# Turning the expert tiles' rows: from TensorE transposes to VectorE's 32x32 block transpose

## The chip, the cores and the metric

One core of one Trainium2 chip runs the whole kernel in one launch. The metric is the time of one execution on the device in microseconds (us), lower is better. A profile is one more execution, recorded instruction by instruction. The engines are named as in the profile: PE is TensorE (PEld its weight loads), DVE is VectorE, ACT is ScalarE, POOL is GpSimd, SP is SyncE, which here only issues DMAs.

## What is computed

The reference is two gated residual layers over `x` of shape (16, 256, 512), all float32. The first is an mLSTM attention, whose part of the kernel the change does not touch. The second is a mixture of experts, for T = 4096 tokens of width H = 512, with E = 16 experts of inner width I = 256 and the best 2 experts of each token:

```
scores = softmax(x @ router_w.T);  topk_w, topk_idx = top_k(scores, 2);  topk_w /= sum(topk_w)
g = einsum('th,ehi->tei', x, expert_gate);  u = einsum('th,ehi->tei', x, expert_up)
a = silu(g) * u
y = einsum('tei,eih,te->th', a, expert_down, gates)
s = silu(x @ shared_gate) * (x @ shared_up) @ shared_down
out = x + tanh(g_ffn) * (y + s)
```

## The kernel before

The kernel has three stages. Stage 1 (0 to about 620 us of the span) goes over the 16 batches: attention, router, the shared expert, and a scatter of each token's normalized row to two places of `routed_x` in HBM, so that the rows of one expert lie together. Stage 2, the expert stage (about 620 to 1027 us), takes those rows in 79 tiles of 128 tokens. Stage 3 combines the experts' outputs with the rest and does the shared expert of four batches that were put off.

Every engine has its own program, written out by hand, and runs it in that order. An instruction that waits for a semaphore holds up all that stand behind it on its engine. The semaphores are counted by tile (`t.n`).

A product of full float32 accuracy is made of three float32r products: an operand is split in a rounded high part and a low part, which is the rest, and the three are high x high, high x low, low x high (`PARTS`). So an activation that goes into a product is first turned (features onto partitions), rounded by one engine, and the rest is made by another.

For a tile `t` of the expert stage the steps are:

- `load_tile` (SP; the first four by ACT at L912): one DMA of 128 rows of 2 KB into `xt`, a ring of four.
- `turn_rows` (PE, L1248): four 128x128 transposes into PSUM bank `t.par`.
- `copy_x` (ACT, L917): PSUM to `xtT[:, 0]`, rounded. `rest_x` (DVE, L1829): PSUM minus that, to `xtT[:, 1]`.
- `gate_up` (PE, L1260): 12 products (four 128-feature chunks `c`, three parts each) into bank 2 or 3.
- `tanh_gate` (ACT, L921) and `silu` (DVE, L1811, L1815) give the activation `act_a`.
- `turn_act` (PE, L1269): two transposes; `copy_actT` (DVE, L1822, L1824): its high and low part.
- `down` (PE, L1278): six products; `copy_y` (ACT, L927) and `store_y` (ACT's DMA queue).

One step of PE is: `turn_rows(t+2)`, `turn_act(t)`, `gate_up(t+1)`, `down(t)`. One step of DVE is: `copy_actT(t)`, `rest_x(t+2)`, `silu(t+1)`.

The weights of expert `e` are loaded by POOL's DMAs into a staging area and split by POOL itself into the ring `w_ring` of two experts: a multiplication by one that rounds (L648), then a subtraction for the low part (L651), each over 128x3072 elements. POOL starts when the last `down` of expert `e-2` is done. The parts of experts 0 and 1 are made before the loop by ACT, DVE (L1805) and POOL (L631, L634):

```
g.tensor_tensor(w_ring[:, k, 0, :], stage[k], one[:, :].to_broadcast([P, EW]), ALU.mult)
g.tensor_tensor(w_ring[:, k, 1, :], stage[k], w_ring[:, k, 0, :], ALU.subtract)
```

Between its second and third step DVE also makes the table of places of the outputs once (seven short operations, L1845 to L1855, "the slot steps").

## Time and profile before

| | us |
|---|---|
| Time, median of 3 runs (lowest, highest) | 1141.49 (1140.75, 1142.49) |
| Span of the profiled execution | 1133.2 |
| Median less span: what lies around the span | 8.3 |
| PE busy | 1025.1 (90% of the span) |
| DVE busy | 761.3 (67%) |
| POOL busy | 419.3 (37%) |
| ACT busy | 386.4 (34%) |

The profiled execution has no time of its own beside its span; 8.3 us is the difference to the median of the timed runs, and a change of the span is taken as the same change of the time. Matmuls overlap in the pipeline, so the busy time of PE says that it never stood idle, not that it did useful work all the time. The page's releasers are inferred: a wait is put down to the event that came last.

### The profile page before, as it was taken

Reading aid. Unit: us, or ns where it says so; the run is one execution under the profiler, and the core shown is the slowest. Engines: PE = TensorE matmul, PEld = TensorE weight load, DVE = VectorE, ACT = ScalarE, POOL = GpSimd, SP = SyncE. Lnnn points to the kernel's source line nnn. Section 1 sums busy time; section 2 is a strip of 40 time slices with the busy share of each in tenths; the row PEclk is TensorE's granted clock in tenths of the full one; section 3 lists DMA queues with packets and bytes.
Section 4 is the critical chain, followed back from the end, with each engine's and each line's share of the span. In section 5 each row is a group of like instructions: output and inputs, shape, how many; then the busy total and the mean of one; then the engine's idle time right before and its main releaser. Section 6 shows DMA issues by size and latency. Waiting matters only on the chain.

```text
span 1133.2 us, 20738 instructions
## 1 busy us (share of the span) xinstructions
PE 1025.1 (90%) x6395; PEld 859.9 (76%) x6395; DVE 761.3 (67%) x1983; ACT 386.4 (34%) x854; POOL 419.3 (37%) x309
## 2 busy tenths in 40 slices
PE   4689999999999988989895599999999999999882
PEld 2578988898889877868684478888888888887661
DVE  2888889888888887878766544444444444444766
ACT  2644444444443444435421123233323333231010
POOL 4010221222112221222215536558656676204675
PEclk9889999999999998989976899999999999999986
DMA  7340210222012202120107744564555554836888
GB/s 259 149 164 1 76 71 9 82 75 76 20 56 76 75 38 80 52 94 38 75 38 260 265 135 167 176 207 158 170 195 193 168 176 149 325 112 186 285 288 272
DMA packets 60036, 155.60 MB, mean 137 GB/s; under 512 B 7296, under 2 KB 7296, under 8 KB 58016
## 3 DMA queue, kind: packets, MB, share of 16 engines
q0 software_dynamic: 18448, 69.22, 17.6%
q1 hardware_dynamic: 29008, 62.93, 16.1%
q10 hardware_dynamic: 12480, 22.16, 5.5%
q8 instruction: 59, 0.97, 0.4%
q14 instruction: 41, 0.34, 0.1%
HBM read 93.46 MB, written 60.82 MB: 136 GB/s over the span
## 4 chain that ended last, share of the span: by engine, by line
PE 80%; DVE 5%; issue 4%; DMA 4%; POOL 3%; ACT 2%; SPq 1%; ACTq 0%; POOLq 0%; DVEq 0%; another core or an unknown queue 0%
PE bank L1260 19%; PE bank L1125 12%; PE bank L1278 10%; PE bank L1030 5%; PE bank L1136 5%; PE bank L1053 4%; PE bank L993 4%; PE bank L1248 3%; POOL w_ring L694 3%; PE bank L1074 3%; PE bank L1077 3%; PE bank L1075 3%; PE bank L1322 2%; PE bank L1062 2%; PE bank L1269 2%
## 5 line engine op out<-in xcount | busy, mean ns | idle before, releaser
L1260 PE MATMUL bank<-w_ring,x2nT 128*128 x948 | 241.8, 404 | 1.7 <-DVE x2nT L1829 1.7
L1260 PEld LDWEIGHTS bank<-w_ring,x2nT 128*128 128x128 f32 x948 | 174.3, 191 | 37.7 <-issue 2.4
L1125 PE MATMUL bank<-x2nT,w_ring 128*128 128x256 f32 x1152 | 148.5, 285 | 0.0
L563 POOL DMA_INDIRECT routed_x<-x2n,slot_u x64 | 65.8, 1029 | 222.8 <-DVE slot_u L1593 207.0
L1125 PEld LDWEIGHTS bank<-x2nT,w_ring 128*128 128x128 f32 x1152 | 141.0, 191 | 0.3
L1811 DVE SCALAR_TENSOR_TENSOR ctxT<-ctxT,bank 128x256 f32<-128x256 f32 x79 | 33.3, 421 | 138.7 <-ACT ctxT L921 138.7
L1278 PE MATMUL bank<-w_ring,sh_actT 128*128 x474 | 123.7, 396 | 1.1 <-DVE sh_actT L1824 1.1
L648 POOL TENSOR_TENSOR w_ring<-area,one 128x3072 fp32r<-128x3072 f32 x14 | 74.2, 5303 | 115.5 <-PE bank L1278 115.5
L1278 PEld LDWEIGHTS bank<-w_ring,sh_actT 128*128 128x128 f32 x474 | 88.9, 188 | 22.5 <-issue 1.4
L651 POOL TENSOR_TENSOR w_ring<-area,w_ring 128x3072 fp32r<-128x3072 f32 x14 | 95.6, 6832 | 2.5 <-POOL w_ring L648 2.5
L921 ACT ACTIVATE ctxT<-bank 128x256 f32<-128x256 f32 x79 | 30.3, 384 | 189.9 <-PE bank L1260 189.9
L694 POOL DMA_INDIRECT w_ring<-routed_y,y_slot x64 | 66.5, 1039 | 34.9 <-issue 19.6
L1136 PE MATMUL bank<-w_ring,sh_actT 128*128 128x512 f32 x288 | 75.2, 411 | 1.3 <-issue 1.3
L1455 DVE SCALAR_TENSOR_TENSOR area<-bank,area 128x384 f32<-128x384 f32 x128 | 66.0, 551 | 14.5 <-PE bank L1053 7.8
L927 ACT COPY cs_in<-bank 128x512 f32<-128x512 f32 x79 | 46.3, 586 | 84.7 <-PE bank L1278 79.1
L1822 DVE CAST sh_actT<-bank 128x256 fp32r<-128x256 f32 x79 | 33.5, 424 | 60.9 <-PE bank L1269 60.9
L570 POOL TENSOR_TENSOR x_rstd<-x_var,minus_half 128x2 f32<-128x2 f32 x16 | 12.8, 797 | 152.4 <-DVE x_var L1518 152.4
L1053 PE MATMUL bank<-area,ctxT 64*128 64x256 f32 (+1 forms) x512 | 67.1, 379 | 0.0
L778 ACT ACTIVATE area<-bank,key_log 128x256 f32<-128x256 f32 x128 | 61.1, 478 | 10.8 <-PE bank L1064 10.2
L1136 PEld LDWEIGHTS bank<-w_ring,sh_actT 128*128 128x128 f32 x288 | 53.8, 194 | 13.0 <-issue 1.5
L1248 PE MATMUL bank<-ident,x2n 128*128 128x128 f32 x316 | 48.4, 277 | 12.5 <-issue 7.0
L1053 PEld LDWEIGHTS bank<-area,ctxT 64*128 64x128 f32 x512 | 51.0, 206 | 11.3 <-issue 5.5
(224 smaller groups left out, 2052.8 us busy)
## 6 DMA issues: line engine op xcount, KB each, us to landing
routed_y<-cs_in ACTq DMA_DIRECT2D x79, 256.0 KB, 2.3
x2n<-routed_x SPq DMA_DIRECT2D x75, 256.0 KB, 2.9
base_out<-in_x_dram SPq DMA_DIRECT2D x16, 512.0 KB, 5.0
cs_in<-in_ctx_dram SPq DMA_DIRECT2D x16, 512.0 KB, 4.0
area<-n_L_ffn_expert_gate_dram POOLq DMA_DIRECT2D x16, 512.0 KB, 4.7
area<-in_L_ffn_expert_up_dram POOLq DMA_DIRECT2D x16, 512.0 KB, 6.3
area<-n_L_ffn_expert_down_dram POOLq DMA_DIRECT2D x16, 512.0 KB, 7.7
out_dram<-base_out SPq DMA_DIRECT2D x32, 256.0 KB
```

Source lines behind the costliest of these rows:

```text
L563: pool.indirect_dma_start(out=routed_x, in_=x2n[:, b.par, j, :], in_offset=None, out_offset=bass.IndirectOffsetOnAxis(ap=slot_u[:, b.par, ...
L648: g.tensor_tensor(w_ring[:, k, 0, :], stage[k], one[:, :].to_broadcast([P, EW]), ALU.mult).then_inc(expert_hi_in.sem, 1)
L651: g.tensor_tensor(w_ring[:, k, 1, :], stage[k], w_ring[:, k, 0, :], ALU.subtract).then_inc(expert_in.sem, 1)
L694: pool.indirect_dma_start(out=y_in[k][:, c, :], in_=routed_y, out_offset=None, in_offset=bass.IndirectOffsetOnAxis(ap=y_slot[:, at:at + 1] ...
L778: s.activation(decay[:, k, 0:S], MB[k][:, 0:S], ACT.Exp, bias=key_log[:, b.par, 0, h:h + 1], scale=-1.0)
L1053: last = mm(QK[k][:, at:at + n], ctxT[half, b.par, q, frm:frm + P], xnT[half, b.par, q, S - n:S], start=True, stop=True)
L1125: last = mm(gu_bank(b.n, m)[:, at:at + S], w[:, w_part, c, m * P:(m + 1) * P], x2nT[:, x_part, c, :], start=(c + p == 0), stop=(c == DC - ...
L1136: last = mm(FF[:, :], sh_actT[:, x_part, m, j * P:(j + 1) * P], sh_down[:, w_part, m, :], start=(m + p == 0), stop=(m == SC - 1 and p == 2))
L1248: last = tr(bank[t.par][:, c * P:(c + 1) * P], xt[:, k, c * P:(c + 1) * P], ident[:, :])
L1260: last = mm(bank[2 + t.par][:, :], xtT[:, x_part, t.par, c * P:(c + 1) * P], w_gu[:, bass.ds(slot, 1), w_part, c, :].rearrange("p a i -> p ...
L1278: last = mm(bank[5 + t.par][:, :], act_aT[:, x_part, t.par, c * P:(c + 1) * P], w_dn[:, bass.ds(slot, 1), w_part, c, :].rearrange("p a i - ...
L1455: v.scalar_tensor_tensor(cmat[:, k, :], QK[k][:, 0:TRI], QK_SCALE, decay[:, k, :], ALU.mult, ALU.mult).then_inc(c_made.sem, 1)
```

## The change

Each tile's rows are loaded by four DMAs instead of one. Quarter `q` takes 128 of the 512 features of all 128 tokens, in pieces of 512 bytes, onto the 32 partitions from `32 q` on. DVE then turns the tile with one block transpose (32x32 blocks) from SBUF to SBUF, into one of two buffers: the new `xt_t`, or `sh_act`, which stage 1 no longer needs. Afterwards partition `p` holds the features `4 p` to `4 p + 3` instead of `p`, `p + 128`, ..., so the rows of the gate and up weights are dealt to the partitions in the same way. `copy_x` and `rest_x` read the SBUF buffer instead of a PSUM bank. On PE `turn_rows` is gone, and the first quarter of `gate_up(t+1)` stands ahead of `turn_act(t)`. On DVE `turn_rows(t+3)` stands between `rest_x(t+2)` and `silu(t+1)`.

```diff
-        xt_in = [event(f"xt_in{k}", 16) for k in range(XRING)]
+        xt_in = [event(f"xt_in{k}", 16 * NQ) for k in range(XRING)]
+        xt_t = (sb("xt_t", [P, D])[:, :], sh_act[:, :, :].rearrange("p a s -> p (a s)"))
+        def load_rows(eng, row, k):
+            for q in range(NQ):
+                own = slice(q * QP, (q + 1) * QP)
+                eng.dma_start(xt[own, k, :].rearrange("t (g n) -> t g n", g=P // QP),
+                              routed_x[bass.ds(row, P), q * P:(q + 1) * P].rearrange("(g t) n -> t g n", t=QP)
+                              ).then_inc(xt_in[k].sem, 16)
...
-                sp.dma_start(xt[:, k, :], routed_x[bass.ds(row, P), :]).then_inc(xt_in[k].sem, 16)
+                load_rows(sp, row, k)
...
-                    src = of[bass.ds(e, 1)].rearrange("a (c p) i -> (a p) c i", p=P)
+                    src = of[bass.ds(e, 1)].rearrange("a (p c) i -> (a p) c i", p=P)
...
             def copy_x(t):
                 act.wait_ge(xt_turned.sem, xt_turned.upto(t.n))
-                s.copy(xtT[:, 0, t.par, :], bank[t.par][:, :]).then_inc(xtT_made.sem, 1)
+                act.wait_ge(gu_made.sem, gu_made.upto(t.n - 2))
+                s.copy(xtT[:, 0, t.par, :], xt_t[t.par]).then_inc(xtT_made.sem, 1)
...
-            def turn_rows(n, t, k):
-                pe.wait_ge(xt_in[k].sem, n)
-                pe.wait_ge(xt_lo_made.sem, xt_lo_made.upto(t.n - 2))
-                for c in range(DC):
-                    last = tr(bank[t.par][:, c * P:(c + 1) * P], xt[:, k, c * P:(c + 1) * P], ident[:, :])
-                last.then_inc(xt_turned.sem, 1)
...
-                if ahead2:
-                    turn_rows(lap * 16 + 16, t + 2, k)
+                    gate_up(t + 1, e, slot, range(0, 1))
                 turn_act(t)
                 if ahead1:
-                    gate_up(t + 1, e, slot)
+                    gate_up(t + 1, e, slot, range(1, DC))
                 down(t)
...
+            def turn_rows(t, k, lap):
+                dve.wait_ge(xt_in[k].sem, xt_in[k].upto(lap))
+                dve.wait_ge(xt_lo_made.sem, xt_lo_made.upto(t.n - 2))
+                v.transpose(xt_t[t.par].rearrange("p (c g t) -> p g c t", c=DC, t=QP),
+                            xt[:, k, :].rearrange("p (g d c) -> p g c d", c=DC, d=QP)).then_inc(xt_turned.sem, 1)
+
             def rest_x(t):
                 dve.wait_ge(xtT_made.sem, xtT_made.upto(t.n))
-                v.tensor_tensor(xtT[:, 1, t.par, :], bank[t.par][:, :], xtT[:, 0, t.par, :], ALU.subtract
+                v.tensor_tensor(xtT[:, 1, t.par, :], xt_t[t.par], xtT[:, 0, t.par, :], ALU.subtract
                                 ).then_inc(xt_lo_made.sem, 1)
 
-            def expert_step(t, ahead2=True, ahead1=True):
+            def expert_step(t, ahead3=True, ahead2=True, ahead1=True):
                 copy_actT(t)
                 if ahead2:
                     rest_x(t + 2)
+                if ahead3:
+                    turn_rows(t + 3, (t.n + 3) % XRING, (t.n + 3) // XRING)
                 if ahead1:
                     silu(t + 1)
```

The instructions that this leaves, by engine, in one step in the middle of the expert stage. A row is a line of the program, the operation, output `<-` inputs and the shape; `x2n` is the ring `xt`, `x2nT` is `xtT`, `ctxT` holds the activation, `sh_actT` is `act_aT`. On PE before, from the last product of one `down` to the first of `gate_up`:

```order
L1278 MATMUL bank<-w_ring,sh_actT 128x512
L1252 TENSOR_LOAD expert_tab
L1252 ISA x2
L1248 MATMUL bank<-ident,x2n 128x128 x4
L1269 MATMUL bank<-ident,ctxT 128x128 x2
L1255 REGISTER_ALU
L1260 ISA
L1260 MATMUL bank<-w_ring,x2nT 128x512 x2
```

The same place on PE now:

```order
L1284 MATMUL bank<-w_ring,sh_actT 128x512
L1256 TENSOR_LOAD expert_tab
L1256 ISA x2
L1260 REGISTER_ALU
L1265 ISA
L1265 MATMUL bank<-w_ring,x2nT 128x512 x2
L1265 ISA
L1265 MATMUL bank<-w_ring,x2nT 128x512
L1275 MATMUL bank<-ident,ctxT 128x128 x2
```

The four row transposes are gone, and three of the twelve gate and up products now stand between `down` and the two transposes of the activation.

One step of DVE before, from `copy_actT` to `silu`:

```order
L1822 CAST sh_actT<-bank 128x256
L1824 TENSOR_TENSOR sh_actT<-bank,sh_actT 128x256
L1829 TENSOR_TENSOR x2nT<-bank,x2nT 128x512
L1811 SCALAR_TENSOR_TENSOR ctxT<-ctxT,bank 128x256
L1815 SCALAR_TENSOR_TENSOR ctxT<-ctxT,bank 128x256
```

The same step of DVE now:

```order
L1820 CAST sh_actT<-bank 128x256
L1822 TENSOR_TENSOR sh_actT<-bank,sh_actT 128x256
L1833 TENSOR_TENSOR x2nT<-xt_t,x2nT 128x512
L1828 STREAM_TRANSPOSE sh_act<-x2n 128x4x4x32
L1809 SCALAR_TENSOR_TENSOR ctxT<-ctxT,bank 128x256
L1813 SCALAR_TENSOR_TENSOR ctxT<-ctxT,bank 128x256
```

A block transpose has come in ahead of `silu`, and the subtraction of `rest_x` has no operand in a PSUM bank any more: both of its inputs (`xt_t` or `sh_act`, and `x2nT`) lie in SBUF.

## Rows read from the trace of the kernel before

**Rows 1.** Expert-stage window: length; busy PE, PEld, DVE, ACT, POOL (instructions); clock; DMA share, GB/s.

```profile
800.00:840.00 40.00, 40.00 (x200) 32.93 (x199) 19.14 (x42) 11.99 (x25) 23.57 (x7) 1.00 0.52 173
```

**Rows 2.** Timeline of one step: start us, us, engine, line, operation, [idle before, releaser].

```profile
804.34 1.36 PEld L1278 LDWEIGHTS bank<-w_ring,sh_actT 128*128 128x128 f32 x6
...
805.19 0.42 DVE L1811 SCALAR_TENSOR_TENSOR ctxT<-ctxT,bank 128x256 f32<-128x256 f32 x1 [1.72 <-ACT ctxT L921]
...
805.75 0.59 PEld L1248 LDWEIGHTS bank<-ident,x2n 128*128 128x128 f32 x4
...
806.30 0.25 PEld L1269 LDWEIGHTS bank<-ident,ctxT 128*128 128x128 f32 x2
...
806.50 5.30 POOL L648 TENSOR_TENSOR w_ring<-area,one 128x3072 fp32r<-128x3072 f32 x1 [8.99 <-PE bank L1278]
806.52 2.62 PEld L1260 LDWEIGHTS bank<-w_ring,x2nT 128*128 128x128 f32 x12
...
806.66 0.59 ACT L917 CAST x2nT<-bank 128x512 fp32r<-128x512 f32 x1
806.83 0.42 DVE L1822 CAST sh_actT<-bank 128x256 fp32r<-128x256 f32 x1 [0.77 <-PE bank L1269]
...
807.63 0.68 DVE L1829 TENSOR_TENSOR x2nT<-bank,x2nT 128x512 fp32r<-128x512 f32 x1
809.18 0.42 PEld L1278 LDWEIGHTS bank<-w_ring,sh_actT 128*128 128x128 f32 x2
```

**Rows 3.** POOL's groups, 640 to 1027 us: busy us, mean ns of one, idle before.

```profile
L651 POOL TENSOR_TENSOR w_ring<-area,w_ring 128x3072 fp32r<-128x3072 f32 x14 | 95.6, 6832 | 2.5 <-POOL w_ring L648 2.5
L648 POOL TENSOR_TENSOR w_ring<-area,one 128x3072 fp32r<-128x3072 f32 x14 | 74.2, 5303 | 115.5 <-PE bank L1278 115.5
```

**Rows 4.** Timeline just before the expert loop, 622 to 634 us.

```profile
622.72 5.30 POOL L631 TENSOR_TENSOR w_ring<-area,one 128x3072 fp32r<-128x3072 f32 x1 [2.85 <-PE bank L1136]
623.33 7.90 DVE L1805 TENSOR_TENSOR w_ring<-area,w_ring 128x3072 fp32r<-128x3072 f32 x1
...
633.27 1.07 ACT L917 CAST x2nT<-bank 128x512 fp32r<-128x512 f32 x2 [18.23 <-PE bank L1248]
```

**Rows 5.** DVE lines: count, ns min/median/max, first and last start.

```profile
L1829 DVE TENSOR_TENSOR x2nT<-bank,x2nT x79: 678/681/692, 633.9 to 1015.8; 128x512 fp32r<-128x512 f32 x79
L1848 DVE TENSOR_TENSOR cs_in<-all_hot,shift x1: 1224/1224/1224, 650.5 to 650.5; 128x1024 f32<-128x1024 bf16 x1
L1607 DVE SCALAR_TENSOR_TENSOR sh_actT<-sh_act,sh_actT x48: 412/416/1881, 90.1 to 604.6; 128x256 fp32r<-128x256 f32 x48
L1405 DVE TENSOR_SCALAR xn<-base_out,ln_mv,ln_rstd x32: 535/541/548, 13.6 to 536.7; 128x512 f32<-128x512 f32 x32
L1421 DVE TENSOR_TENSOR_SCAN f_row<-one,f_row x16: 678/679/681, 28.8 to 551.2; 8x256 f32<-8x256 f32 x16
```

**Rows 6.** Timeline of stage 1, 126 to 129 us, DVE and POOL.

```profile
126.70 0.96 POOL L563 DMA_INDIRECT routed_x<-x2n,slot_u  x1 [0.30 <-issue]
...
127.12 1.88 DVE L1607 SCALAR_TENSOR_TENSOR sh_actT<-sh_act,sh_actT 128x256 fp32r<-128x256 f32 x1
127.65 1.06 POOL L553 COPY area<-cs_in 128x1024 f32<-128x1024 f32 x1
```

**Rows 7.** Windows of stage 3, an idle stretch of PE and what follows; columns as rows 1.

```profile
1060.40:1063.10 2.70, 0.14 (x2) 0.06 (x1) 1.99 (x4) 0.00 (x0) 2.09 (x3) 1.00 1.05 407
...
1064.40:1067.90 3.50, 3.50 (x13) 2.74 (x11) 1.41 (x2) 0.54 (x1) 2.81 (x3) 0.51 0.96 315
```

**Rows 8.** Start of the expert loop: DVE's slot steps, and PE after an idle stretch.

```profile
650.07 0.17 DVE L1845 TENSOR_SCALAR shift<-tile_first 128x16 f32<-128x16 f32 x1
...
653.49 0.25 DVE L1855 TENSOR_SCALAR all_w<-all_w,tanh_g 128x64 f32<-128x64 f32 x1
654.37 0.66 PE L1248 MATMUL bank<-ident,x2n 128*128 128x128 f32 x4 [4.14 <-DMA x2n<-routed_x]
```

**Rows 9.** The four row loads that ACT issues: ns min/median/max.

```profile
L912 ACTq DMA_DIRECT2D x2n<-routed_x x4: 344/371/411, 626.0 to 632.9; - x4
```

More of the change, by code:

```diff
@@ L50 @@
 YRING = 4
+QP = 32
+NQ = P // QP
 LATE_LOADS = [9, 16]
@@ L543, in load_expert @@
                 dn = stage[k][:, DC * 2 * I:EW].rearrange("p (c d) -> p c d", c=IC)
-                sides = ((gu[:, :, 0:I], expert_gate, DC), (gu[:, :, I:2 * I], expert_up, DC), (dn, expert_down, IC))
-                for to, of, c in sides:
-                    src = of[bass.ds(e, 1)].rearrange("a (c p) i -> (a p) c i", p=P)
+                for to, of in ((gu[:, :, 0:I], expert_gate), (gu[:, :, I:2 * I], expert_up)):
+                    src = of[bass.ds(e, 1)].rearrange("a (p c) i -> (a p) c i", p=P)
                     pool.dma_start(to, src).then_inc(expert_dma[k].sem, 16)
+                src = expert_down[bass.ds(e, 1)].rearrange("a (c p) i -> (a p) c i", p=P)
+                pool.dma_start(dn, src).then_inc(expert_dma[k].sem, 16)
             def values(b):
@@ L911, in _ @@
                 row = act.value_load(row_tab[0:1, n:n + 1], min_val=0, max_val=DUMP)
-                act.dma_start(xt[:, n, :], routed_x[bass.ds(row, P), :]).then_inc(xt_in[n].sem, 16)
+                load_rows(act, row, n)
             def copy_x(t):
                 act.wait_ge(xt_turned.sem, xt_turned.upto(t.n))
-                s.copy(xtT[:, 0, t.par, :], bank[t.par][:, :]).then_inc(xtT_made.sem, 1)
+                act.wait_ge(gu_made.sem, gu_made.upto(t.n - 2))
+                s.copy(xtT[:, 0, t.par, :], xt_t[t.par]).then_inc(xtT_made.sem, 1)
             def tanh_gate(t):
@@ L1240, in _, with gate_up @@
             shared_down(Item(0, LAST), 1)
-            def turn_rows(n, t, k):
-                pe.wait_ge(xt_in[k].sem, n)
-                pe.wait_ge(xt_lo_made.sem, xt_lo_made.upto(t.n - 2))
-                for c in range(DC):
-                    last = tr(bank[t.par][:, c * P:(c + 1) * P], xt[:, k, c * P:(c + 1) * P], ident[:, :])
-                last.then_inc(xt_turned.sem, 1)
             def expert_of(t):
                 return pe.value_load(expert_tab[0:1, bass.ds(t.n, 1)], min_val=0, max_val=E - 1)
-            def gate_up(t, e, slot):
-                pe.wait_ge(expert_in.sem, e + 1)
-                pe.wait_ge(xt_lo_made.sem, xt_lo_made.upto(t.n))
-                pe.wait_ge(act_made.sem, act_made.upto(t.n - 2))
-                for c in range(DC):
+            def gate_up(t, e, slot, of):
+                if of[0] == 0:
+                    pe.wait_ge(expert_in.sem, e + 1)
+                    pe.wait_ge(xt_lo_made.sem, xt_lo_made.upto(t.n))
+                    pe.wait_ge(act_made.sem, act_made.upto(t.n - 2))
+                for c in of:
                     for p, (w_part, x_part) in enumerate(PARTS):
@@ L1262, in gate_up @@
                                   start=(c + p == 0), stop=(c == DC - 1 and p == 2))
-                last.then_inc(gu_made.sem, 1)
+                if of[-1] == DC - 1:
+                    last.then_inc(gu_made.sem, 1)
             def turn_act(t):
@@ L1296, in _ @@
             pe.wait_ge(tables_made.sem, tables_made.upto(0))
-            turn_rows(16, Item(0, 0), 0)
-            turn_rows(16, Item(0, 1), 1)
             e = expert_of(Item(0, 0))
-            gate_up(Item(0, 0), e, pe.snap(e % RING))
-            expert_step(Item(0, 0), 2, 0)
-            expert_step(Item(0, 1), 3, 0)
-            for n in range(2, TILES - 2):
-                expert_step(Item(0, n), (n + 2) % XRING, (n + 2) // XRING)
-            for n in range(TILES - 2, TILES):
-                expert_step(Item(0, n), 0, 0, ahead2=False, ahead1=n + 1 < TILES)
+            gate_up(Item(0, 0), e, pe.snap(e % RING), range(DC))
+            for n in range(TILES):
+                expert_step(Item(0, n), ahead1=n + 1 < TILES)
             def late_gate_up(u, k):
@@ L1835, in expert_step @@
                     rest_x(t + 2)
+                if ahead3:
+                    turn_rows(t + 3, (t.n + 3) % XRING, (t.n + 3) // XRING)
                 if ahead1:
                     silu(t + 1)
+            turn_rows(Item(0, 0), 0, 0)
+            turn_rows(Item(0, 1), 1, 0)
             rest_x(Item(0, 0))
+            turn_rows(Item(0, 2), 2, 0)
             rest_x(Item(0, 1))
@@ L1856, in _ @@
             assert steps[0] == TABLE_STEPS + SLOT_STEPS
-            for n in range(2, TILES - 2):
-                expert_step(Item(0, n))
-            expert_step(Item(0, TILES - 2), ahead2=False)
-            expert_step(Item(0, TILES - 1), ahead2=False, ahead1=False)
+            for n in range(2, TILES):
+                expert_step(Item(0, n), ahead3=n + 3 < TILES, ahead2=n + 2 < TILES, ahead1=n + 1 < TILES)
             dve.wait_ge(base_made.sem, base_made.upto(SH[LAST]))
```

2 lines of the change are left out of this document (1 added, 1 removed).

## Prediction

> **What bounds the kernel now.** I read the times by engine first, then the windows by stage, then one step of the expert stage instruction by instruction. In the expert stage PE is never idle: 40.00 of 40.00 us at granted clock 1.00, the 2.4 GHz level, while DVE is busy 19.14 us and ACT 11.99 [rows 1]. So a tile costs what PE's instructions cost. The timeline of one step [rows 2] gives the shares by the starts of PE's weight loads, which follow each other without a gap: `down` 804.34 to 805.75 (1.41 us), row transposes to 806.30 (0.55), activation transposes to 806.52 (0.22), `gate_up` to 809.18 (2.66), together 4.84 us.
>
> Two more things are to be seen in that step. First, DVE has room but little of it at the right moment: `silu` (two operations, 0.42 us each, the first at 805.19, 0.85 us after `gate_up` ended) is done at about 806.07 and `turn_act` could start at 806.30, 0.23 us later. The row transposes are what PE does meanwhile. Second, POOL begins its split of the next expert 0.75 us after `down` ends (806.50 against 805.75) and is then busy for 5.30 and 6.83 us; it does so 14 times [rows 3], once for each expert from 2 to 15, 2.5 / 14 = 0.18 us between the two halves.
>
> **What the change removes.** The row transposes: 0.55 us of PE's 4.84 by the weight loads. By the matmuls' own starts it could be 0.44, since boundaries between kinds of instructions take some of it; I take 0.50. Of 79 tiles the first three are turned while PE waits for other things, so 76 x 0.50 = 38 us (33 to 42).
>
> **What it puts in their place on PE.** A quarter of `gate_up` (2.66 / 4 = 0.67 us) now covers `silu`, in place of 0.55 us of transposes. The slack at `turn_act` becomes 0.23 + 0.12 = 0.35 us.
>
> **What it adds to DVE.** A block transpose of 128x512, of which the trace has no instance. Below it is bounded by the nearest single-input operation from SBUF of that size, L1405 with 0.54 us; above by an operation that takes twice the usual time an element, the scan L1421 (0.68 us for 256 elements against 0.41 for the plain operation L1607, which makes some 1.3 us for 512) [rows 5]. I take 0.68 us, as `rest_x` (L1829) takes for the same 512 elements, because both are one pass over them. In an undisturbed step this is free: counted from the start A of `turn_act`'s weight loads, `rest_x` starts at A + 1.33 us (807.63 less 806.30 [rows 2]) and ends at A + 2.01; the transpose ends at A + 2.7; the next `silu` cannot start before A + 0.22 + 2.00 + 0.85 = A + 3.07 (rest of `gate_up`, then ACT's tanh). With PE's 0.35 us, a transpose of up to 1.4 us hides.
>
> **What it changes in `rest_x`.** This is the term that decides. Before, one input lies in PSUM. L1829 took 678 to 692 ns in all 79 instances [rows 5], although POOL was splitting for 28 stretches of 5 to 7 us meanwhile. Now both inputs lie in SBUF. The trace has this operation once beside a POOL split: L1805, a subtraction of the same kind with 3072 elements, starts at 623.33 and takes 7.90 us, while POOL's L631 runs from 622.72 to 628.02 [rows 4]. Alone it should take about 3.3 us: 1.22 us for 1024 elements [rows 5], 0.54 us less for 512, so some 1.06 ns an element. And 628.02 + 3.3 = 631.3, while it ended at 631.23. So DVE did not run slower beside POOL: it stood still until POOL's instruction was over.
>
> So after the change, with 0 at the end of a tile's `gate_up`, in the step in which an expert's last `down` ends: `down` to 1.41, the quarter to 2.08 = A, POOL's L648 from 1.41 + 0.75 = 2.16 to 7.46. `rest_x` wants to start at A + 1.33 = 3.41 and stands until 7.46, 4.05 us. The transpose and `silu` are queued behind it on DVE; `silu` starts at 7.46 + 0.68 + 0.68 = 8.82 instead of A + 3.07 = 5.15, 3.67 us late; less the slack of 0.35, PE stands 3.3 us at `turn_act`. L651 then starts at 8.14 (ready at 7.64, but now `rest_x` holds it up) and ends at 14.97. PE's next `turn_act` starts at 6.38 + 3.3 = 9.7, the next `rest_x` wants 11.0 and stands until 14.97, 3.9 us: PE stands another 3.2. The third `rest_x` is free. That is 6.5 us for each of 14 experts: 92 us. The split of an expert must be done one expert later, 4 x 4.3 + 6.5 = 23.7 us or more, so POOL, with 12.8 us for it, is not late itself.
>
> The Trainium skill has a rule on this order of events (SBUF — State Buffer, SBUF: two separate sides): the read and write ports that VectorE and GpSimd share are an exclusive lock, and whoever starts first has it for the whole instruction. By that rule `rest_x`, first in line when L648 ends, goes ahead of L651, which is the 92 us above; if it did not, the cost would be that of the second rival below.
>
> **The clock.** An idle stretch of PE can cost more than its length. In stage 3 PE was busy 0.14 us in 2.70, and from 1.3 us later on the granted clock stood at 0.51, the 1.2 GHz level, for 3.5 us [rows 7]. At half speed 3.4 us hold 1.7 us of work less. After an expert's first stall that is absorbed by the second (the end of L651 sets the time). After the second it counts. I take half of 14 x 1.7 = 24 us: 12 (0 to 24).
>
> **The rest.** `copy_x` reads SBUF, on ACT, which starts it at 806.66, some 1 us ahead of `rest_x`; if it took more than 0.4 us longer, `rest_x` would move, and the 1.4 us above is what absorbs it. SP issues four DMAs a tile instead of one, each 0.34 to 0.41 us [rows 9]: 1.2 us more in a step of 4.3 in which SP does nothing else, and the rows are loaded some four steps (17 us) ahead; without that cover a tile would wait the whole landing. The dealt weight rows move the same bytes by the same number of DMAs, under POOL's wait of 115.5 / 14 = 8 us [rows 3]. At the start, ACT issues 16 loads instead of four before it reaches `copy_x`: 12 x (0.37 + 0.08 for registers) = 5.4 us, so `gate_up(0)` comes 5 us later. Then PE waited 4.14 us for the fifth tile's rows anyway [rows 8], so most of this is covered. But DVE now waits for those rows itself, ahead of `silu(2)`, and behind that stand the slot steps (650.07 to 653.74, 3.7 us), which lay under PE's wait before. Together I put 2.5 us on it (0 to 6).
>
> **Sum.** -38 + 92 + 12 + 2.5 = +68 us. The span goes from 1133.2 to some 1201, and the time from the median of 1141.5 to 1210 us.
>
> **The rivals.** *DVE is not held up by POOL.* Then only the saving remains, -38 + 2.5: 1106 us. For it speaks that L1805 is one instance; against it that its end fits to 0.1 us, and that L1607, also with both inputs in SBUF, takes up to 1.88 us instead of 0.42 where POOL works [rows 5, 6]. It decides if a wait of `rest_x` beside L648 stays under 0.7 us. Chance 0.09.
>
> *One long stall instead of two short ones.* In stage 1, L1607 stood through POOL's L563 and then through L553 right behind it, from 127.12 to 129.00 [rows 6]: a waiting DVE may be passed over. If so, `rest_x` stands from 3.41 to the end of L651 at 14.47, 11.1 us, and PE 10.4. The same comes out if the block transpose itself needs what POOL holds: `rest_x` slips in at 7.46, L651 starts at 8.14, the transpose stands until 14.97, and PE stands 10 us. 14 x 10 to 10.4, with the clock falling each time (24), gives -38 + 2.5 + 143 + 24: 1273 us. Chance 0.20.
> The Trainium skill says (DVE: opcode table, instruction layouts, handler registers and perf-mode slots, Perf-mode slots) that an operation with one float32 source can run in the mode that uses both ports. If that holds for the transpose, it is the second form of this rival; no row here has a transpose.
>
> *A slow transpose.* At 1.3 us each blocked step costs 0.6 us more, 28 x 0.6 = 17: 1227 us; above 1.4 us every step would lengthen. Chance 0.07 for 1225 to 1275.
>
> *Half of it hides*, because `rest_x` in many experts meets the gap, or PE keeps more slack than I count: 1150 to 1185 us. Chance 0.08.
>
> **How the numbers follow.** The forecast has 0.56, with 1185 to 1235 as its own range (its saving, clock and start at their bounds). A measurement can tell a change from none at about 0.2% (2.3 us). Faster 0.10 is the first rival and a little of what hides; within 0.2% 0.02; slower 0.88. The range from 1165 to 1262 holds the forecast, two thirds of what hides, most of the slow transpose and, with the clock steady, part of the long stall: some 0.78.
>
> **What would show it.** `rest_x` (two SBUF inputs) with a minimum near 0.68 us and 28 instances of 4 to 5 us, each ending where POOL's L648 or L651 ends; PE idle before `turn_act` about 3 us, 28 times, released by DVE's `silu`; steps without a split near 4.3 us; granted clock under 1.00 in the expert stage, where it was 1.00. I am wrong if `rest_x` stays at 0.68 us throughout, if it stands through both halves of a split, or if the transposes take more than 1.4 us.

## The result, and the profile after

The changed kernel takes 1198.12 us (median of four runs, 1194.35 to 1198.98) against 1141.3 us of the kernel before in the same comparison: a ratio of 1.0494, with a 95% interval from 1.0468 to 1.052. That is 56.8 us more. The forecast was 1210 us, with 1185 to 1235 as its own range.

The groups of the costliest instructions show the cause that was forecast. Columns: busy us in all, mean ns of one, idle time before and its releaser.

```profile
L659 POOL TENSOR_TENSOR w_ring<-area,one 128x3072 fp32r<-128x3072 f32 x14 | 74.2, 5302 | 169.3 <-PE bank L1284 169.3
...
L662 POOL TENSOR_TENSOR w_ring<-area,w_ring 128x3072 fp32r<-128x3072 f32 x14 | 98.2, 7013 | 2.5 <-POOL w_ring L659 2.5
...
L1833 DVE TENSOR_TENSOR x2nT<-xt_t,x2nT 128x512 fp32r<-128x512 f32 x40 | 77.1, 1926 | 6.5 <-ACT x2nT L929 6.5
...
L1833 DVE TENSOR_TENSOR x2nT<-sh_act,x2nT 128x512 fp32r<-128x512 f32 x39 | 74.2, 1901 | 0.0
```

`rest_x` (L1833; before it was L1829 [rows 5]) now has a mean of 1.9 us. POOL's first half of the split is unchanged, the second takes 7.01 us in place of 6.83 [rows 3]. The views of the two new or changed lines of DVE give minimum, median and maximum in ns:

```profile
L1833 DVE TENSOR_TENSOR x2nT<-xt_t,x2nT x40: 681/682/4455, 644.7 to 1078.0; 128x512 fp32r<-128x512 f32 x40
L1833 DVE TENSOR_TENSOR x2nT<-sh_act,x2nT x39: 647/682/4459, 646.6 to 1073.6; 128x512 fp32r<-128x512 f32 x39
```

```profile
L1828 DVE STREAM_TRANSPOSE xt_t<-x2n x40: 1068/1084/1102, 636.1 to 1074.2; 128x512 f32<-128x512 f32 x40
```

The median of `rest_x` is what it was, 0.68 us; those beside a split take up to 4.46 us. The block transpose takes 1.07 to 1.10 us in every instance. The timeline of one expert's split shows where the long instances lie (start us, length us, engine; in brackets the idle time before and its releaser):

```profile
838.40 5.30 POOL L659 TENSOR_TENSOR w_ring<-area,one 128x3072 fp32r<-128x3072 f32 x1 [12.45 <-PE bank L1284]
...
839.79 4.45 DVE L1833 TENSOR_TENSOR x2nT<-sh_act,x2nT 128x512 fp32r<-128x512 f32 x1
...
843.88 7.01 POOL L662 TENSOR_TENSOR w_ring<-area,w_ring 128x3072 fp32r<-128x3072 f32 x1 [0.18 <-POOL w_ring L659]
844.17 1.09 DVE L1828 STREAM_TRANSPOSE xt_t<-x2n 128x512 f32<-128x512 f32 x1
...
844.51 0.96 PE L1265 MATMUL bank<-w_ring,x2nT 128*128 x3 [2.08 <-issue]
...
846.07 0.44 PE L1275 MATMUL bank<-ident,ctxT 128*128 128x128 f32 x2 [0.61 <-DVE ctxT L1813]
...
847.35 4.09 DVE L1833 TENSOR_TENSOR x2nT<-xt_t,x2nT 128x512 fp32r<-128x512 f32 x1
...
851.36 1.07 DVE L1828 STREAM_TRANSPOSE sh_act<-x2n 128x512 f32<-128x512 f32 x1
...
851.70 0.96 PE L1265 MATMUL bank<-w_ring,x2nT 128*128 x3 [1.73 <-POOL w_ring L662]
...
853.24 0.44 PE L1275 MATMUL bank<-ident,ctxT 128*128 128x128 f32 x2 [0.58 <-DVE ctxT L1813]
...
854.52 0.68 DVE L1833 TENSOR_TENSOR x2nT<-sh_act,x2nT 128x512 fp32r<-128x512 f32 x1
```

The first long `rest_x` ends at 844.24, 0.54 us after POOL's first half (843.70); the second ends at 851.44, 0.55 us after its second half (850.89). It is the same for all 14 experts: 28 instances end 0.55 us (547 to 553 ns) after the POOL instruction that they started beside. PE stands twice in each stall: at the first quarter of `gate_up` (L1265), which needs that `rest_x`, and then at `turn_act` (L1275), which needs `silu`: 2.08 + 0.61 and 1.73 + 0.58 us. The name POOL at 851.70 is an inference; what ends just then is the long `rest_x`. The third `rest_x` meets no POOL instruction and takes 0.68 us.

The starts of `down`, one for each tile, give the length of every step. Of the steps from the fourth `down` on they are 4.39 us where POOL does not split (4.84 before, [rows 2]), and in each of 14 experts two neighbours are long. The differences between the starts of `down` in that stretch of the trace (us, worked out):

```
expert after expert:  7.55+7.16  7.49+8.75  8.49+6.21  8.63+6.00  8.41+6.31  8.51+6.13  7.54+7.16
                      7.50+8.67  9.00+5.72  8.63+6.04  8.40+6.31  8.55+6.09  8.74+5.93  8.95+5.71
```

Twelve pairs have 14.6 to 14.7 us, 5.9 more than two plain steps, and two have 16.2. Together that is 85.7 us.

The granted clock, 1.00 from the fourth to the last `down` before, fell in that stretch to its 1.2 GHz level 12 times, for 3.4 us each. Two such places, then the whole stretch, now and in the kernel before, with the columns of rows 1 (the clock is the third figure from the end):

```profile
895.00:902.00 7.00, 4.31 (x14) 2.93 (x13) 6.15 (x7) 1.20 (x2) 6.82 (x2) 0.78 0.24 76
...
926.00:929.60 3.60, 3.14 (x10) 2.17 (x9) 2.75 (x6) 0.62 (x1) 3.60 (x1) 0.53 0.43 129
```

```profile
671.88:1086.58 414.70, 358.14 (x1490) 270.29 (x1488) 337.40 (x446) 113.42 (x223) 203.23 (x71) 0.95 0.50 156
```

```profile
664.22:1025.42 361.20, 360.06 (x1782) 295.94 (x1780) 170.59 (x373) 108.45 (x223) 200.48 (x71) 1.00 0.52 179
```

The kernel before needed 361.20 us for this stretch.

The start, too, is longer. The timeline of the first steps:

```profile
623.46 0.27 DVE L1797 CAST expert_tab<-bank 1x128 int32<-1x128 f32 x1
...
631.25 12.74 ACTq L402 DMA_DIRECT2D x2n<-routed_x  x16
...
644.09 0.62 ACT L929 CAST x2nT<-xt_t 128x512 fp32r<-128x512 f32 x1 [24.24 <-DMA routed_x<-xn]
...
660.76 1.08 DVE L1828 STREAM_TRANSPOSE xt_t<-x2n 128x512 f32<-128x512 f32 x1 [2.48 <-DMA x2n<-routed_x]
...
662.64 0.44 PE L1275 MATMUL bank<-ident,ctxT 128*128 128x128 f32 x2 [1.72 <-DVE ctxT L1813]
...
667.31 1.66 PE L1284 MATMUL bank<-w_ring,sh_actT 128*128 x6 [2.17 <-DVE sh_actT L1822]
```

ACT issues 16 loads in 12.74 us and only then starts `copy_x`, 20.6 us after the tables are made (623.46); before, that took 14.7 us (618.55 to 633.27). The fifth tile's rows hold DVE at 660.76, with `silu` behind them (PE stands 1.72 us), and the slot steps behind that hold `copy_actT` (PE stands 2.17 us).

One caution on the spans: before the change the profiled execution has a span 8.3 us under the median, after it 1.7 us. In the profile of before the tables are made at 618.55 us, in that of after at 623.46, although the program is the same up to there. So spans are compared from that point on: 514.7 us before, 572.9 after, 58.3 more.

### The profile page after: what moved, and what is told of

The parts are those of the page before. It is cut to its first block, busy times and chain, and to the rows that moved or that the text cites. A ratio compares the mean times of both kernels' runs of the same rounds, so it can differ in the third digit from the quotient of the medians.

```text
span 1196.4 us, 20975 instructions
## 1 busy us (share of the span) xinstructions
PE 1027.4 (86%) x6079; PEld 837.9 (70%) x6079; DVE 937.1 (78%) x2062; ACT 391.4 (33%) x854; POOL 422.2 (35%) x309
## 3 DMA queue, kind: packets, MB, share of 16 engines
q1 hardware_dynamic: 61408, 62.94, 16.2%
## 4 chain that ended last, share of the span: by engine, by line
PE 67%; DVE 19%; issue 5%; DMA 4%; POOL 2%; SPq 1%; ACT 1%; ACTq 0%; POOLq 0%; DVEq 0%
PE bank L1265 12%; PE bank L1137 12%; DVE x2nT L1833 9%; PE bank L1284 6%; PE bank L1042 5%; PE bank L1148 4%; PE bank L1005 4%; PE bank L1065 4%; PE bank L1320 3%; PE bank L1086 3%; PE bank L1087 2%; PE bank L1089 2%; PE bank L1275 2%; PE bank L1074 2%; POOL w_ring L705 2%
## 5 line engine op out<-in xcount | busy, mean ns | idle before, releaser
L1265 PE MATMUL bank<-w_ring,x2nT 128*128 x948 | 270.1, 425 | 59.5 <-issue 50.1
L1265 PEld LDWEIGHTS bank<-w_ring,x2nT 128*128 128x128 f32 x948 | 181.2, 201 | 108.1 <-issue 73.8
L1137 PE MATMUL bank<-x2nT,w_ring 128*128 128x256 f32 x1152 | 153.3, 291 | 0.0
L1137 PEld LDWEIGHTS bank<-x2nT,w_ring 128*128 128x128 f32 x1152 | 146.0, 198 | 0.3
L659 POOL TENSOR_TENSOR w_ring<-area,one 128x3072 fp32r<-128x3072 f32 x14 | 74.2, 5302 | 169.3 <-PE bank L1284 169.3
L662 POOL TENSOR_TENSOR w_ring<-area,w_ring 128x3072 fp32r<-128x3072 f32 x14 | 98.2, 7013 | 2.5 <-POOL w_ring L659 2.5
L1833 DVE TENSOR_TENSOR x2nT<-xt_t,x2nT 128x512 fp32r<-128x512 f32 x40 | 77.1, 1926 | 6.5 <-ACT x2nT L929 6.5
L1833 DVE TENSOR_TENSOR x2nT<-sh_act,x2nT 128x512 fp32r<-128x512 f32 x39 | 74.2, 1901 | 0.0
L1086 PE MATMUL bank<-area 128*128 128x65 f32 x256 | 51.6, 285 | 9.5 <-DVE area L1453 8.6
```

The source lines that it names most:

```text
L1086: mm(HO[:, r:r + VW], cmat[:, k, 0:P], v_aug[:, b.par, 0, h, :], start=True, stop=True)
L1137: last = mm(gu_bank(b.n, m)[:, at:at + S], w[:, w_part, c, m * P:(m + 1) * P], x2nT[:, x_part, c, :], start=(c + p == 0), stop=(c == DC - ...
L1265: last = mm(bank[2 + t.par][:, :], xtT[:, x_part, t.par, c * P:(c + 1) * P], w_gu[:, bass.ds(slot, 1), w_part, c, :].rearrange("p a i -> p ...
L1833: v.tensor_tensor(xtT[:, 1, t.par, :], xt_t[t.par], xtT[:, 0, t.par, :], ALU.subtract).then_inc(xt_lo_made.sem, 1)
```

## The experiments

The theory: `rest_x` stands until POOL's instruction ends because both its inputs lie in SBUF. The rivals: the transposes on DVE, the loads, or the clock make the loss. The table gives the times, their ratios to the kernel before in the same comparison (its median lies between 1139.9 and 1145.1 us), and from each profile the time from the tables to the fourth `down` and from there to the 79th, from the starts of L1797 and of `down`.

| kernel | time, us | ratio to before (95%) | tables to 4th `down` | 4th to 79th `down` |
|---|---|---|---|---|
| before | 1141.3 | | 45.7 | 361.2 |
| after | 1198.12 | 1.0494 (1.0468 to 1.052) | 48.4 | 414.7 |
| 1 transpose into PSUM | 1117.2 | 0.978 (0.9751 to 0.9809) | 48.3 | 331.5 |
| 2 before, `rest_x` from SBUF | 1205.39 | 1.0554 (1.0527 to 1.0582) | 46.4 | 426.0 |
| 3 POOL's split in pieces | 1133.3 | 0.9925 (0.9903 to 0.9948) | 49.3 | 352.1 |
| 4 as 1, ACT's start | 1114.77 | 0.978 (0.9745 to 0.9816) | 48.3 | 331.4 |
| 5 `silu` ahead of the transpose | 1185.69 | 1.0399 (1.0347 to 1.0451) | 49.3 | 402.9 |
| 6 as 1, plain blocks | 1112.93 | one run | 48.0 | 330.5 |
| 7 as 1, one load a tile | 1108.82 | 0.9728 (0.9681 to 0.9776) | 47.2 | 329.8 |
| 8 as 4, slot steps spread | 1128.22 | 0.9872 (0.983 to 0.9914) | 44.5 | 347.6 |
| 9 as 4, start written out | 1106.58 | 0.9682 (0.9636 to 0.9728) | 44.6 | 331.5 |
| 10 the first again | 1115.59 | 0.974 (0.9693 to 0.9788) | 48.0 | 331.7 |

**1. The transpose writes PSUM.**

```diff
-                s.copy(xtT[:, 0, t.par, :], xt_t[t.par]).then_inc(xtT_made.sem, 1)
+                s.copy(xtT[:, 0, t.par, :], bank[t.par][:, :]).then_inc(xtT_made.sem, 1)
...
-                v.transpose(xt_t[t.par].rearrange("p (c g t) -> p g c t", c=DC, t=QP),
+                v.transpose(bank[t.par][:, :].rearrange("p (c g t) -> p g c t", c=DC, t=QP),
...
-                v.tensor_tensor(xtT[:, 1, t.par, :], xt_t[t.par], xtT[:, 0, t.par, :], ALU.subtract
+                v.tensor_tensor(xtT[:, 1, t.par, :], bank[t.par][:, :], xtT[:, 0, t.par, :], ALU.subtract
```

> The changed kernel, but VectorE's block transpose writes into the PSUM bank that TensorE's transposes used, and copy_x and rest_x read that bank; nothing else differs, so rest_x again has one SBUF input. Theory (rest_x with two SBUF inputs stands until POOL's instruction ends): rest_x is near 0.68 us in all instances, the steps beside a split go from a pair of 14.7 us to 8.8, and the time is 1198 less 14 x 5.9 to 6.1 us = 1112 to 1116 us, below the kernel before. Rival (the transpose's 1.08 us on VectorE ahead of silu, or the four small-row loads a tile, make the stall): the pairs stay near 14 us and the time over 1180 us. Half and half, some 1150 us, would say that the transpose waits as well once it writes PSUM.

Measured: 1117.2 us, 80.9 below the changed kernel and 24.5 below the kernel before. The views of the two lines in its trace:

```profile
L1833 DVE TENSOR_TENSOR x2nT<-bank,x2nT x79: 665/681/692, 648.2 to 999.3; 128x512 fp32r<-128x512 f32 x79
```

```profile
L1828 DVE STREAM_TRANSPOSE bank<-x2n x79: 1081/1102/1125, 640.8 to 995.5; 128x512 f32<-128x512 f32 x79
```

All 79 `rest_x` take 0.67 to 0.69 us, and every step beside a split is 4.39 us long. The stretch is 83.2 us shorter: the 85.7 us of the long pairs are gone, and two steps near its end, of 5.54 and 6.20 us, bring 3.0 us back. The transpose, the loads and the order on PE are as in the changed kernel, so the transpose's 1.1 us are hidden, and the stalls came from where its result lies. This version beats both kernels.

**2. The kernel before with that input in SBUF.**

```diff
-                v.tensor_tensor(xtT[:, 1, t.par, :], bank[t.par][:, :], xtT[:, 0, t.par, :], ALU.subtract
+                v.tensor_tensor(xtT[:, 1, t.par, :], sh_act[:, :, :].rearrange("p a s -> p (a s)"), xtT[:, 0, t.par, :], ALU.subtract
```

> The kernel before, TensorE's transposes kept; only rest_x takes its first input from a tile of the same size that lies still in SBUF (sh_act) instead of the PSUM bank, so its result is not the rounding rest of the rows. Theory: the wait comes with the second SBUF input alone. Per expert the stall is that of the changed kernel (5.9 us) less the two transposes queued ahead of silu there (2 x 1.08) plus two slacks smaller by 0.12: 4.0 us, so 14 x 4.0 = 56 us and a time near 1197 us (1180 to 1215). Rival (transposes or loads make the stall): at most 1150 us, rest_x near 0.68 us.

Measured: 1205.39 us, 63.7 above the kernel before and within the range that was expected. Its timeline around one split:

```profile
680.60 5.30 POOL L648 TENSOR_TENSOR w_ring<-area,one 128x3072 fp32r<-128x3072 f32 x1 [29.18 <-PE bank L1278]
...
681.74 4.72 DVE L1829 TENSOR_TENSOR x2nT<-sh_act,x2nT 128x512 fp32r<-128x512 f32 x1
...
686.08 6.98 POOL L651 TENSOR_TENSOR w_ring<-area,w_ring 128x3072 fp32r<-128x3072 f32 x1 [0.18 <-POOL w_ring L648]
687.29 0.44 PE L1269 MATMUL bank<-ident,ctxT 128*128 128x128 f32 x2 [1.77 <-DVE ctxT L1815]
...
688.57 5.05 DVE L1829 TENSOR_TENSOR x2nT<-sh_act,x2nT 128x512 fp32r<-128x512 f32 x1
```

One operand alone brings the two long instances, 4.7 and 5.1 us, without a block transpose and without the finer loads. Most pairs are 14.1 to 14.2 us long, 4.4 to 4.5 over two steps of 4.84 (4.0 was expected); two have 15.5 and 15.7 us, with a fall of the clock behind them. Runs 1 and 2 together settle the cause.

**3. POOL's split in pieces.**

```diff
-                g.tensor_tensor(w_ring[:, k, 1, :], stage[k], w_ring[:, k, 0, :], ALU.subtract
-                                ).then_inc(expert_in.sem, 1)
+                for q in range(4):
+                    own = slice(q * EW // 4, (q + 1) * EW // 4)
+                    last = g.tensor_tensor(w_ring[:, k, 1, own], stage[k][:, own], w_ring[:, k, 0, own], ALU.subtract)
+                last.then_inc(expert_in.sem, 1)
```

The first half is cut in the same way.

> The changed kernel with each of POOL's two split instructions cut into four of 768 columns (1.33 and 1.71 us by their lengths). Theory (the wait lasts for POOL's running instruction, and VectorE is served before POOL's next one): rest_x takes at most 2.4 us, each stall shrinks to 0 to 1.4 us, no gap is followed by a half clock, and the time is 1198 - 85 + 14 x (0.5 to 2.5) = 1120 to 1148 us. Rival (a waiting VectorE is passed over by POOL's next piece): rest_x still takes 4 to 11 us and the time stays at 1190 us or more.

Measured: 1133.3 us, as the theory has it. The view of `rest_x` and POOL's groups:

```profile
L1838 DVE TENSOR_TENSOR x2nT<-xt_t,x2nT x40: 681/692/2203, 643.0 to 1015.1; 128x512 fp32r<-128x512 f32 x40
```

```profile
L661 POOL TENSOR_TENSOR w_ring<-area,one 128x768 fp32r<-128x768 f32 x56 | 87.0, 1582 | 83.0 <-PE bank L1289 83.0
L667 POOL TENSOR_TENSOR w_ring<-area,w_ring 128x768 fp32r<-128x768 f32 x56 | 112.9, 2045 | 2.5 <-POOL w_ring L661 2.5
```

The longest `rest_x` is 2.20 us, 1.52 more than alone, about one piece: a waiting VectorE is served between two instructions of POOL. Against the first run the stretch still loses 20.6 us, 1.5 for each expert. POOL pays as well: 56 pieces of each half take 87.0 and 112.9 us, where 14 whole ones took 74.2 and 98.2.

**4. ACT's order at the start.**

```diff
-            for n in range(XRING):
+            def load_first(n):
...
+            load_first(0)
+            load_first(1)
             copy_x(Item(0, 0))
+            load_first(2)
             copy_x(Item(0, 1))
+            load_first(3)
```

VectorE turns tile 2 behind the second `rest_x`.

> The kernel of the first run with the first tiles' order changed: ACT issues the eight loads of tiles 0 and 1, then the rounding copy of tile 0, the four loads of tile 2, the copy of tile 1, the four loads of tile 3; VectorE turns tile 2 behind rest_x of tile 1. Theory (the expert stage starts late because ACT issues 16 loads ahead of its first copy): the first gate_up starts 3 to 5 us earlier than in the first run and the time is 3 to 5 us below it. Rival (the stage's second step waits for the slot steps and the fifth tile's rows anyway): the first gate_up moves but the second step takes back as much; within 1 us of the first run.

Measured: 1114.77 us with the same ratio as the first run. The first `gate_up` starts 15.5 us after the tables in place of 21.0, but the fourth `down` 48.27 in place of 48.30: the second and third step give all of it back. The rival held. What costs at the start is not ACT's 16 loads.

**5. `silu` ahead of the transpose.**

```diff
-                if ahead3:
-                    turn_rows(t + 3, (t.n + 3) % XRING, (t.n + 3) // XRING)
                 if ahead1:
                     silu(t + 1)
+                if ahead3:
+                    turn_rows(t + 3, (t.n + 3) % XRING, (t.n + 3) // XRING)
```

> The changed kernel with one edit: in each step VectorE computes silu ahead of the block transpose instead of behind it; rest_x keeps its two SBUF inputs. The prediction's reading (PE stands at turn_act for silu, so that all that is queued ahead of silu counts in full): each of 28 stalls shrinks by the transpose's 1.08 us, 30 us, to 1165 to 1171 us. Rival (PE stands mostly at the first quarter of gate_up, which waits for rest_x itself; only the second, shorter gap, 0.6 us before turn_act, is silu's): 28 x 0.6 = 17 us, to 1179 to 1184 us. If neither gap is silu's, it stays within 3 us of 1198.

Measured: 1185.69 us, 12.4 below the changed kernel: less than either figure. Its timeline around one split:

```profile
677.88 4.46 DVE L1833 TENSOR_TENSOR x2nT<-sh_act,x2nT 128x512 fp32r<-128x512 f32 x1
...
682.60 0.95 PE L1265 MATMUL bank<-w_ring,x2nT 128*128 x3 [2.08 <-issue]
...
683.39 0.38 PE L1275 MATMUL bank<-ident,ctxT 128*128 128x128 f32 x2
...
684.83 4.71 DVE L1833 TENSOR_TENSOR x2nT<-xt_t,x2nT 128x512 fp32r<-128x512 f32 x1
...
689.79 0.95 PE L1265 MATMUL bank<-w_ring,x2nT 128*128 x3 [2.55 <-POOL w_ring L662]
```

The gap before `turn_act` is gone at 683.39, as the rival has it. But the next `rest_x` starts sooner and stands longer (4.71 in place of 4.09 us), and the next gap is 2.55 in place of 1.73 us, since its end is set by the end of POOL's second half, which did not move. So what is saved in the first stall is given back in the second; per expert 0.84 us remain in the mean (11.8 / 14), where two gaps of 0.6 had been counted.

**6. Blocks with elements side by side.**

```diff
-                            xt[:, k, :].rearrange("p (g d c) -> p g c d", c=DC, d=QP)).then_inc(xt_turned.sem, 1)
+                            xt[:, k, :].rearrange("p (g c d) -> p g c d", c=DC, d=QP)).then_inc(xt_turned.sem, 1)
```

> The kernel of the first run, with the block transpose reading each block's 32 elements side by side instead of 16 bytes apart; the rows' columns then come out in another order than the weights', so the output is another. Theory (the step of 16 bytes between elements makes the transpose take 1.08 us where one pass over 512 elements takes 0.68): 0.6 to 0.75 us. Rival (the transpose itself costs that, whatever the step): 1.05 to 1.12 us. The time of the kernel should not move by either, since the transpose hides: within 3 us of the first run.

```profile
L1828 DVE STREAM_TRANSPOSE bank<-x2n x79: 714/715/727, 634.9 to 988.4; 128x512 f32<-128x512 f32 x79
```

The transpose takes 0.715 us in place of 1.10: the step of 16 bytes between the elements costs 0.39 us. The kernel's time (1112.93 us, one run) does not tell itself from the first run's, so the transpose is hidden at either length.

**7. One load a tile.**

```diff
-            for q in range(NQ):
...
+            eng.dma_start(xt[:, k, :], routed_x[bass.ds(row, P), :]).then_inc(xt_in[k].sem, 16)
```

> The kernel of the first run, with each tile's rows loaded by one DMA of whole 2 KB rows as before the change, instead of four of 512-byte pieces; the block transpose then leaves the blocks in the wrong places, so the output is another. Theory (the fourfold loads cost at the start, where the fifth tile's rows land late, and at the end, where two steps of 5.5 and 6.2 us stand beside the late weights' loads): the third down comes 1 to 3 us earlier after the tables are made, all steps from the fifth on take 4.4 us (3 us less), together 4 to 6 us below the first run. Rival (the loads are hidden): within 1.5 us of the first run.

Measured: 1108.82 us. The third `down` starts 42.21 us after the tables, as in the first run (42.23), though the first `gate_up` comes 5.5 us sooner; the fourth starts 47.17 us after them, 1.1 us sooner. The long steps near the end shrink from 5.54 + 6.20 to 5.95 + 4.39, half of what was expected, and the stretch is 1.7 us shorter. Together that is 2.8 us, where 4 to 6 were expected. That leaves most of the 8.4 us between the medians outside the expert stage: in the two profiled executions the tables were made at 628.15 (the first run) and 618.79 us, by the same instructions, and the intervals of the two ratios overlap.

**8. The slot steps spread.** From the fourth run: `silu` ahead of the transpose in all steps, and one slot step behind each of seven tiles.

```diff
             for n in range(2, TILES):
                 expert_step(Item(0, n), ahead3=n + 3 < TILES, ahead2=n + 2 < TILES, ahead1=n + 1 < TILES)
+                if 4 <= n < 4 + len(slot_steps):
+                    then(slot_steps[n - 4]())
```

> The kernel of the fourth run (transpose into PSUM, first tiles' order changed) with silu ahead of the block transpose in each step and the seven slot steps dealt one to a step from the fifth step on. Theory (the start is held by silu queued behind the wait for the fifth tile's rows and by the slot steps behind it): the third down comes 3 to 6 us earlier after the tables are made than in the first and the fourth run, and the time is 1109 to 1113 us, if the transposes' copies, now 0.85 us later, still come in time (steps of 4.4 us). Rival (PE then waits for the fifth tile's rows themselves): the first three steps together take what they took, and the time is within 1.5 us of the fourth run.

Measured: 1128.22 us, a miss, and an instructive one. What was expected of the start came: the third `down` starts 37.3 us after the tables in place of 42.2 and the fourth 44.5 in place of 48.3. But two pairs of steps, 8.38 + 6.97 and 8.33 + 6.94, lose 13 us. The timeline shows what stood there:

```profile
678.61 5.30 POOL L659 TENSOR_TENSOR w_ring<-area,one 128x3072 fp32r<-128x3072 f32 x1 [26.84 <-PE bank L1288]
...
679.12 4.82 DVE L1861 TENSOR_SCALAR shift<-tile_first 128x16 f32<-128x16 f32 x1
...
684.09 6.79 POOL L662 TENSOR_TENSOR w_ring<-area,w_ring 128x3072 fp32r<-128x3072 f32 x1 [0.18 <-POOL w_ring L659]
...
685.07 2.92 PE L1288 MATMUL bank<-w_ring,sh_actT 128*128 x6 [3.84 <-DVE sh_actT L1826]
...
686.16 1.14 DVE L1832 STREAM_TRANSPOSE bank<-x2n 128x512 f32<-128x512 f32 x1
687.20 3.71 DVE L1862 TENSOR_TENSOR shift<-shift,expert_row 128x16 f32<-128x16 f32 x1
...
708.36 4.66 DVE L1868 CAST y_slot<-y_slot_f 128x64 uint32<-128x64 f32 x1
...
716.28 3.69 DVE L1869 TENSOR_SCALAR all_w<-all_w,tanh_g 128x64 f32<-128x64 f32 x1
```

Four small slot steps of 0.17 to 0.26 us fell beside a split and took 3.7 to 4.8 us, each until 0.03 to 0.06 us after the end of POOL's instruction, and `copy_actT` behind the first held PE for 3.84 us. It is the same wait, and operations that read a single tensor (L1861, L1868) are in it too. Three steps near the end of the stretch lose another 2.4 us (5.11 + 7.74 + 5.83 in place of 5.54 + 6.22 + 4.56 in the fourth run); why was not tried.

**9. The start written out.** From the fourth run: `silu` of the second and third tile ahead of the next transpose, and the slot steps behind `copy_actT` of the third tile.

```diff
-            expert_step(Item(0, 0))
-            expert_step(Item(0, 1))
+            copy_actT(Item(0, 0))
+            rest_x(Item(0, 2))
+            silu(Item(0, 1))
+            turn_rows(Item(0, 3), 3, 0)
+            copy_actT(Item(0, 1))
+            rest_x(Item(0, 3))
+            silu(Item(0, 2))
+            copy_actT(Item(0, 2))
...
+            turn_rows(Item(0, 4), 0, 1)
+            rest_x(Item(0, 4))
+            silu(Item(0, 3))
+            turn_rows(Item(0, 5), 1, 1)
```

> The kernel of the fourth run (transpose into PSUM, first tiles' order changed) with VectorE's first steps written out: silu of the second and third tile ahead of the next transpose, and the seven slot steps directly behind copy_actT of the third tile, ahead of the fifth tile's transpose and so under the wait for its rows; from the fourth tile on all as in the first run. Theory (the start costs what stands behind the wait for the fifth tile's rows): the fourth down comes 4 to 7 us earlier after the tables are made than the 48.3 us of the first and the fourth run, no slot step meets a POOL split, and the time is 4 to 7 us below that of the first run in the same comparison. Rival (the rows' landing itself holds PE): the fourth down stays within 1.5 us of 48.3 us, and the time within 2 us.

Measured: 1106.58 us, the lowest time of all, 9.0 below the first version in the same comparison. The fourth `down` starts 44.64 us after the tables, 3.3 us sooner than in run 10 and 3.7 sooner than in run 1, just short of the 4 to 7 us that were expected; the time fell by more than the 4 to 7 us. The other 5 to 6 us do not lie in the expert stage (331.5 and 331.7 us). In the two profiled executions the tables were made at 619.42 and 627.19 us, and the span ended 107.6 and 112.0 us behind the start of the last `down`, by the same instructions; so these 5 to 6 us can't be put down to the edit.

**10. The first version again.**

> The kernel of the first run once more, unchanged, beside the ninth, so that the two are compared on one chip: 1112 to 1118 us, the same steps of 4.39 us beside the splits.

Measured: 1115.59 us, and the same steps of 4.39 us beside the splits.

## Why the prediction came out as it did

The theory stands: undone alone, the loss is gone (run 1); made alone, it is there (run 2); and its size follows the length of POOL's instruction (run 3). The terms of the sum, forecast and measured:

| step of the prediction | forecast, us | measured, us |
|---|---|---|
| row transposes leave PE | -38 (33 to 42) | -34.7: 77 steps x 0.45 |
| two stalls for each of 14 experts | +92 | +82.7: 14 x 5.9 |
| clock | +12 (0 to 24) | +3: two pairs of 16.2 in place of 14.7 |
| start | +2.5 (0 to 6) | +4.1: 48.4 less 45.7, and 3 x 0.45 saved in it |
| not forecast | | +3.1: 1.1 in steps of 4.40 to 4.62 us, 2.0 behind the last `down` |
| sum | +68 | +56.8 by the medians, 58.3 by the traces from the tables on |

Stall and clock were forecast some 18 us too high together, and the other terms took back about 8, so part of the error cancelled. The 2.0 us behind the last `down` (109.8 less 107.8) can't be told from the variation between executions: with the same instructions that stretch took 107.4 to 112.0 us in the profiled executions here.

**The stall** was forecast as two nearly equal stops of 3.3 and 3.2 us. Its mechanism was right, its size a little off: 5.9 for 6.5. The chain from `down` to the end of POOL's second half was put at 14.97 us and took 14.64 (836.25, where the weight loads of `down` start, to 850.89): `rest_x` in between held POOL up for 0.18 us (7.01 for 6.83), not for 0.50 (8.14 less 7.64). And `rest_x` ended 0.55 us after POOL, not 0.68. (The row that the mechanism was read from, L1805, would by the prediction's own slope take 3.4 us alone, 1.22 us and 2048 x 1.06 ns, not 3.3; so its end fits to 0.2 us, not to 0.1.) Where PE stands was not quite right: the prediction has it wait at `turn_act` alone, for `silu`. It waits first at the quarter of `gate_up` ahead of it, whose rows are that same late `rest_x`; so the sign that was named, PE idle for about 3 us before `turn_act`, did not come: there it is 0.6 us, and 1.7 to 2.1 us stand before the quarter where the clock did not fall. So the queue behind `rest_x` counts less than was said: the transpose came out 0.4 us longer than taken without lengthening the stall, and moving `silu` ahead of it (run 5) gave 0.84 us for an expert, not 2 x 1.08.

**The clock** fell nearly as often as was feared, 12 times for 14 experts, and cost a quarter. Ten of the 12 slow stretches follow the first stall of an expert, and their pairs are no longer than those without one (8.49 + 6.21 and 7.54 + 7.16): the second stall ends with POOL's second half, whatever PE lost before it. Only the two behind a second stall cost, 1.5 us each. The prediction said so, and then took half of all.

**The transposes.** A step saves 0.45 us, at the matmuls' own starts and not at the weight loads' (0.44 and 0.55 were the two readings; 0.50 was taken).

**The block transpose** was valued by the row of a plain pass, 0.68 us. With elements side by side that is right (0.715 us in run 6); the program reads them 16 bytes apart, and so it is 1.08. Within 1.4 us it hides, as forecast: in run 1 it takes 1.10 us and the steps are 4.39. The Trainium skill has a rule that fits (SBUF — State Buffer, Door 1: The DMA port swizzle): consecutive accesses within one 16-byte line go at full rate, and each that crosses to a new line pays. The trace agrees with it, 1.10 against 0.715 us; other steps than 16 bytes were not tried.

**The start** was read rightly, place by place: the gain of an earlier `gate_up` is swallowed by the wait for the fifth tile's rows, and `silu` and the slot steps behind that wait are new on the path. Runs 4 and 7 show the first: of a `gate_up` that comes 5.5 us sooner, nothing and 1.1 us are left at the fourth `down`. Run 9 shows the second, and recovers 3.3 of the 4.1 us.

**The frame.** The 8.3 us between span and median were carried over to the changed kernel; there they are 1.7. In all other runs the time of a profiled execution is 1.5 to 1.9 us above its span, so most of the 8.3 us presumably did not lie around the span: the profiled execution of before was quick in stage 1 (tables at 618.55 us, 623.46 after; 618.8 to 628.2 in all the others). The total is 57 to 58 us by either reckoning.

**The rivals.** "DVE is not held up" falls by run 2. "One long stall" falls in both its forms: `rest_x` goes ahead of POOL's second half (843.70 to 844.24), and the block transpose at 844.17 runs beside it in 1.09 us. "Half of it hides" does not occur: all 14 experts stall. "A slow transpose" does not either: 1.10 us at most, under the 1.4 us that hide.

## What to carry to other kernels

An operand that moves from PSUM to SBUF can cost more than the work it saves: before such a move, look on the VectorE side for operations that would then read and write SBUF alone, and on the GpSimd side for long instructions that run meanwhile. Here the same change with the transpose's result in PSUM is worth -24.5 us in place of +56.8. Where the operand can't stay in PSUM, short GpSimd instructions bound the wait (1.5 us in place of 3.8), and where a wait is set by the end of another engine's long instruction, nothing that is saved ahead of that end counts.
